# Adding up scan states: transfers that accumulate take one add of each pair, and the maxima of attention become a strand of their own

## The reference, cut to what matters

```python
dA  = exp(dt[..., None] * A)
dBx = (dt * xi)[..., None] * Bm[:, :, None, :]
def step(h, inp):
    a, bx, c = inp
    h = a * h + bx
    return (h, einsum('bds,bs->bd', h, c))
y = ys + xi * Dp
```

```python
m = max(sim, axis=-1);  e = exp(sim - m);  out = (e @ v) / sum(e)
```

## Time and profile before

| | |
|---|---|
| median of 3 runs | 3390.97 us |
| profiled execution | 3388.55 us, span 3386.7 us |
| busy share PE / DVE / ACT / POOL | 77% / 76% / 48% / 49% |
| mean granted TensorE clock | 0.802 |
| DMA engines' share, bytes | 23.4%, 253.07 MB |

### The profile page before, as it was taken

One profiled execution on the slowest core, in us unless ns is written; L12 is line 12 of the kernel. 1 busy time (PEld: TensorE's weight loads), 2 busy tenths in 40 slices (PEclk: granted clock), 3 DMA queues, 4 the chain that ended last, 5 costly groups with the idle time before them and its releaser, 6 DMA issues.

```text
span 3386.7 us, 29269 instructions
## 1 busy us (share of the span) xinstructions
PE 2602.9 (77%) x8306; PEld 846.3 (25%) x8306; DVE 2563.1 (76%) x3658; ACT 1642.3 (48%) x2312; POOL 1645.2 (49%) x1349
## 2 busy tenths in 40 slices
PE   5414465878788887988789977998589878988886
PEld 1101121223222332223222321233122322232211
DVE  1688899888788879887988888887988786346251
ACT  3434444563737474464547364556436442532523
POOL 1377676574626475455626474545736561112111
PEclk7656576799979996798779886898679876988867
DMA  2122222222313132132312231232313230102111
GB/s 80 55 81 67 76 89 88 61 87 85 101 44 92 61 117 81 64 97 70 116 38 92 83 114 55 70 91 71 124 54 107 69 109 20 60 28 80 45 35 32
DMA packets 160658, 253.07 MB, mean 75 GB/s; under 512 B 20720, under 2 KB 58480, under 8 KB 160240
## 3 DMA queue, kind: packets, MB, share of 16 engines
q1 hardware_dynamic: 160496, 251.19, 23.4%
HBM read 233.81 MB, written 16.52 MB: 74 GB/s over the span
## 4 chain that ended last, share of the span: by engine, by line
PE 46%; DVE 31%; ACT 11%; issue 8%; POOL 2%; DMA 1%; SPq 1%; DVEq 0%; POOLq 0%; ACTq 0%
PE ps L488 46%; DVE rh L1213 8%; DVE nmx L1133 5%; DVE xib L1192 3%; ACT tN L1448 3%; ACT ps L1502 2%; DVE xif L1192 2%; DVE rh L1219 2%; ACT L1250 1%; DVE tF L1074 1%; DVE tF L1079 1%; DVE tL L1121 1%; SPq L1657 1%; POOL tF L1578 1%; DVE duf L1002 0%
## 5 line engine op out<-in xcount | busy, mean ns | idle before, releaser
L1213 DVE TENSOR_TENSOR_SCAN rh<-ps,rb 128x512 f32<-128x512 f32 x512 | 622.6, 1216 | 122.4 <-ACT ps L1502 105.3
L1547 POOL TENSOR_TENSOR rh<-rh,cs 128x512 f32<-128x512 f32 x256 | 381.1, 1491 | 448.6 <-DVE rh L1213 448.5
L1133 DVE TENSOR_REDUCE nmx<-ps 128x1 f32<-128x512 f32 (+3 forms) x864 | 528.1, 660 | 59.5 <-PE ps L488 57.2
L1448 ACT ACTIVATE tN<-ps 128x1024 f32<-128x1024 f32 (+1 forms) x448 | 429.7, 959 | 258.1 <-PE ps L488 256.4
L488 PE MATMUL ps<-tN,strip 128*64 128x512 f32 (+3 forms) x2048 | 488.2, 568 | 5.3 <-DVE hN L1152 2.9
L1558 POOL TENSOR_TENSOR rb<-duf,bs 128x512 f32<-128x512 f32 x256 | 369.6, 1462 | 137.2 <-DVE rh L1213 127.8
L488 PE MATMUL ps<-hF,W 128*128 128x512 f32 x592 | 367.9, 707 | 73.1 <-DVE tF L1074 44.4
L1558 POOL TENSOR_TENSOR rb<-dub,bs 128x512 f32<-128x512 f32 x256 | 376.0, 1489 | 81.4 <-DVE rh L1213 81.0
L488 PE MATMUL ps<-Ks,Qs 48*128 48x512 bf16 (+3 forms) x1024 | 332.5, 416 | 83.8 <-DVE nmx L1133 69.1
L1572 POOL TENSOR_TENSOR tF<-tF,cr 128x512 f32<-128x512 f32 x128 | 168.7, 1320 | 392.1 <-DVE tF L1079 235.1
L488 PE MATMUL ps<-tF,W 128*128 128x512 f32 x544 | 311.6, 669 | 23.4 <-POOL tF L1578 18.2
(11 more groups left out here) (237 smaller groups left out, 3566.1 us busy)
## 6 DMA issues: line engine op xcount, KB each, us to landing
cr<-shares SPq DMA_DIRECT2D x256, 256.0 KB, 3.3
bs<-rowsf SPq DMA_DIRECT2D x128, 256.0 KB, 3.6
cs<-rowsf SPq DMA_DIRECT2D x128, 256.0 KB, 3.3
bs<-rowsb SPq DMA_DIRECT2D x128, 256.0 KB, 3.6
cs<-rowsb SPq DMA_DIRECT2D x128, 256.0 KB, 3.3
parts<-spl SPq DMA_DIRECT2D x32, 384.0 KB, 2.6
Qs<-parts SPq DMA_DIRECT2D x384, 32.0 KB
Ks<-parts SPq DMA_DIRECT2D x384, 32.0 KB
```

Source lines behind the costliest of these rows:

```text
L1133: red(nmx[:, qt, 8 * a + i:8 * a + i + k], o[:, 0:k * nk].rearrange("p (k c) -> p k c", k=k), AX.X, ALU.max, negate=True).then_inc(s_red, 1)
L1213: eng.tensor_tensor_scan(rh[n % NH][:, g, :], PS, rb[n % NBB][:, g, :], 0.0, ALU.mult, ALU.add).then_inc(s_h, 1)
L1448: act(tN[m % NP][:, :, 0:nq], PR[:, :, 0:nq], ACT.Exp).then_inc(s_ex, 1)
L1547: tt(h, h, cs[n % NB][:, :], ALU.mult).then_inc(s_cp, 1)
```

## The change

It has three parts, and the orders of SyncE, TensorE, DVE, ScalarE and POOL are written anew for them.

1. Of the 16 states of a direction, the first 14 are added up in 7 pairs (`NPAIR`). POOL issues a transfer of 128x1024 floats from the even state's tile to the odd state's tile that accumulates (`accum_op=ALU.add`), and DVE adds only the odd one to xi. The last two are added one by one. So DVE makes 9 adds for a direction in place of 16, and POOL issues 7 transfers.
2. NH is 4 in place of 3. The scan of state n now waits for state n-4: for an even one until the pair's transfer has landed (`pair_done`), for an odd one until DVE's add.
3. The maxima are a strand X with their own jobs (`jx`). Their first 8 score tiles use PA[0] and PA[1] alone, and wait, in the first tile of each bank, for the last exponential of the job ahead, not for its x. From the ninth on all three banks are used, and the first tile in PA[2] waits for that x. The output projection goes into PA[2]. The maxima are laid out so that four transfers in place of six carry them to `Qs`, two for each half of the heads, with a semaphore for each half.

```diff
-        NB, NBB, NH = 3, 2, 3
+        NB, NBB, NH = 3, 2, 4
+        NPAIR = 7
+        ADDS = NS - NPAIR
+        def pair_done(k, i):
+            m = NPAIR * k + i
+            return s_pair[m % 2], 16 * (m // 2 + 1)
+        def added(n):
+            k, s = divmod(n, NS)
+            return s_y, ADDS * k + (s // 2 + 1 if s < 2 * NPAIR else s - NPAIR + 1)
+        def state_free(n):
+            k, s = divmod(n, NS)
+            return pair_done(k, s // 2) if s < 2 * NPAIR and s % 2 == 0 else added(n)
+        FIRST = 8
+        def bank_of(u):
+            return u % 2 if u < FIRST else (2, 0, 1)[(u - FIRST) % 3]
...
+            def maxima(j, l3, before):
...
-                    if u >= 3:
-                        eng.wait_ge(s_red, tops_of(n) + u - 2)
-                    o, k = PA[u % 3], len(pieces)
+                    if last_in_bank(u) is not None:
+                        eng.wait_ge(s_red, tops_of(n) + last_in_bank(u) + 1)
+                    elif n:
+                        eng.wait_ge(*(before.dve("x") if bank_of(u) == 2 else (s_ex, units_of(n))))
+                    o, k = PA[bank_of(u)], len(pieces)
...
-                    if e == 0:
-                        eng.wait_ge(s_nm, 96 * (n + 1))
+                    if 2 * e % len(UNITS[l3]) == 0:
+                        eng.wait_ge(s_nm[g], 32 * (n + 1))
...
-                mm(R0, w(name + "o"), hN[:, :]).then_inc(*A.by_pe(j, "o"))
+                mm(O, w(name + "o"), hN[:, :]).then_inc(*A.by_pe(j, "o"))
...
                 def add_state(n):
                     k, p, s = SEQ[n]
-                    eng.wait_ge(*times_c_done(n))
-                    if s:
-                        eng.wait_ge(s_y, n)
+                    if s < 2 * NPAIR:
+                        eng.wait_ge(*pair_done(n // NS, s // 2))
                     else:
+                        eng.wait_ge(*times_c_done(n))
...
                         if n >= NH:
-                            eng.wait_ge(s_y, n - NH + 1)
+                            eng.wait_ge(*state_free(n - NH))
...
-                    if s >= 1:
-                        add_state(n - 1)
+                    if s % 2 == 0 and s >= 4:
+                        add_state(n - 3)
                         yield
                     if s == NS - 1:
-                        add_state(n)
-                        yield
+                        for m in (n - 2, n - 1, n):
+                            add_state(m)
+                            yield
...
+                def add_pair(n):
+                    k, i = n // NS, n % NS // 2
+                    eng.wait_ge(*times_c_done(n))
+                    eng.wait_ge(*times_c_done(n + 1))
+                    eng.dma_start(rh[(n + 1) % NH][:, :, :], rh[n % NH][:, :, :], accum_op=ALU.add).then_inc(
+                        s_pair[(NPAIR * k + i) % 2], 16)
...
+                    if s % 2 and 3 <= s < 2 * NPAIR + 2:
+                        add_pair(n - 3)
+                        yield
...
-                    for a in range(2):
-                        for m in range(3):
-                            dma(Qs[64 * a + 48 + m:64 * a + 49 + m, :, :],
-                                cTN[16 * m + 8 * a:16 * m + 8 * a + 8, :]).then_inc(s_nm, 16)
+                    for g in range(2):
+                        for a in range(2):
+                            dma(Qs[64 * a + 48:64 * a + 51, 4 * g:4 * g + 4, :],
+                                cTN[24 * g + 12 * a:24 * g + 12 * a + 12, :]).then_inc(s_nm[g], 16)
```

More of the change, by code:

```diff
@@ L164 @@
+        "A1S4A1S10A2S2M1F1S1F1S2F1S1F1S2F1S3F1S1F2S4F3S1F4S1F1S3A1S5A1S1A1S4A1S7A1S1A1S1M1S1A1S6F1S1F1A1S6F2S3F4M1F5A1F"
+        "2A1F1A5F2A1F14A4F1A1F3A1F2A1F2A1F8A1F3A1F5A7F3A1F2A1F3A3F8"
     ),
@@ L199 @@
     "prep3": chain("q k v bdq bdk", "q sqq k sqk v lnq rsq lnk rsk s0q s1q s0k s1k", "nq nk d0q d1q d0k d1k", ln=LN1),
-    "att2": chain("T o", "dl0 dr0 rd0 dl1 dr1 rd1", "n0 n1 n2 n3 ct on0 on1 x", ln={}),
-    "att3": chain("T o", "dl0 dr0 rd0 dl1 dr1 rd1", "n0 n1 n2 n3 ct on0 on1 x", ln={}),
+    "maxima": chain("T", "", "n0 n1 n2 n3 ct", ln={}),
+    "att": chain("o", "dl0 dr0 rd0 dl1 dr1 rd1", "on0 on1 x", ln={}),
 }
@@ L390, in build @@
                     jf[b, n] = Job(F, kind, b)
-            for b, n, kind in ((k - 3, "a3", "att3"), (k - 1, "a2", "att2")):
+            for b, n in ((k - 3, "a3"), (k - 1, "a2")):
                 if 0 <= b < B:
-                    ja[b, n] = Job(A, kind, b)
+                    ja[b, n], jx[b, n] = Job(A, "att", b), Job(X_, "maxima", b)
         for b in range(B):
@@ L472, in weights, with last_in_bank @@
             return [(g, p, t) for g in range(2) for p in range(4) for t in tiles]
+        FIRST = 8
         TOPS, UNITS = [tops(0), tops(1)], [weights(0), weights(1)]
         KINDS_A = [int(n == "a3") for _, n in ja]
+        def bank_of(u):
+            return u % 2 if u < FIRST else (2, 0, 1)[(u - FIRST) % 3]
+        def last_in_bank(u):
+            return max((v for v in range(u) if bank_of(v) == bank_of(u)), default=None)
         def tops_of(n):
@@ L720, in prep @@
                     yield
-            def attention(j, l3):
-                n, name = ATT[j.b, l3], "a3" if l3 else "a2"
-                R0, R1, O = PA
-                for s, v in j.after:
-                    eng.wait_ge(s, v)
-                if j.b == 0:
-                    eng.wait_ge(s_w[5 if l3 else 4], 16)
+            def maxima(j, l3, before):
+                n = ATT[j.b, l3]
                 for u, (pieces, nk) in enumerate(TOPS[l3]):
@@ L778, in values @@
                     eng.wait_ge(s_ex, m + 1)
+                    if e == 0 and n:
+                        eng.wait_ge(*j.after[-1])
                     if e == per:
@@ L830, in strand_f, with strand_x @@
                         yield from (ffn2 if n in ("f0", "f1") else ffn3)(j)
+            def strand_x():
+                before = None
+                for (b, n), j in jx.items():
+                    yield from maxima(j, int(n == "a3"), before)
+                    before = ja[b, n]
             def strand_a():
@@ L1234, in strand_f, with strand_x @@
                         yield from (ffn2 if n in ("f0", "f1") else ffn3)(j)
+            def strand_x():
+                for (b, n), j in jx.items():
+                    yield from maxima(j, int(n == "a3"))
             def strand_a():
```

279 lines of the change are left out of this document (148 added, 131 removed).

## The result

| | before | after |
|---|---|---|
| median of the runs, us | 3393.8 (3386.3 to 3397.4, 4 runs) | 3445.1 (3439.1 to 3451.3, 4 runs) |
| span of the profiled execution, us | 3386.7 | 3442.9 |
| mean granted TensorE clock | 0.802 | 0.790 |
| ratio after / before | | 1.0159 (95%: 1.0140 to 1.0178) |

The change makes the kernel 1.6% slower. (Before has one run more here than in the table ahead of the prediction.) I had said 3295 us, by my sum 97 us faster. The median is outside my range too (3225 to 3410).

What follows compares the result with a forecast made beforehand. No single bound: DVE paces the first stretch, DVE and PE alternate in the middle, PE mostly paces the last. From 3388.55 us, -40 - 65 - 12 - 5 + 25 = -97 gave 3291.6, stated as 3295 us; range 3225 to 3410.

Steps and rivals of the forecast that it cites:

- Part 1, adds: DVE in the scans: 112 fewer adds, 175 us less work, gaining 40 us in the first stretch and 65 in the middle.
- The gains of my sum (40, 65, 12 and 5 us): Fewer adds in the first stretch (40) and middle (65), earlier maxima in the tail (12) and middle (5).
- the transfers' 25 us: Scans waiting for pair transfers: 32 us of waiting, of which 25 us reach the end.
- near 2710: Sign to look for: the last scan begins near 2710 us in place of 2798.
- Part 3, maxima: Attention handovers: 8 reduces begin before the x of the job ahead, gaining 12 us in the tail, 5 in the middle.
- Part 2, the issue on POOL: POOL's 112 transfer issues: at 1 us each, 112 us more on POOL, hidden unless scans wait for its products.
- The rule of the Trainium skill that I weighed: POOL's transfers starved by DVE holding the shared port pair: waiting near 150 us in place of 32, result about 3400.
- Part 2, landing: Pair transfers ahead of scans: 5.5 us landing plus 1 us issue, 32 us of waiting; 91 us if 8 us.
- PE takes over: Rival, middle stretch: DVE's freed time turns idle because PE is at 83%; 3362 us, chance 0.18.
- Late transfers: Rival, first scan of even states: the pair lands late, stalling DVE's queue; near 3475 to 3545 us, chance 0.20.
- Both relieved in full: Rival: gains at full size, -76 - 129 - 30 + 20, giving 3175 us, half way 3230; chance 0.08.
- My own range: The forecast's range, 3240 to 3345 us: middle's term between 20 and 110, transfers' between 0 and 45.

Runs made afterwards that it cites:

- e1: The changed kernel without its 112 accumulating transfers, waits going to the products by C instead; 3292.6 us, 0.9704 of before.
- e13: The kernel before, in its own orders and maxima, with pairs added by POOL's accumulating transfers, issued early, and a POOL wait after each issue; 3360.9 us, 0.9900 of before.
- e11: The changed kernel with each transfer issued ahead of the product by C, and a POOL wait after each issue; 3306.4 us, 0.9743 of before.
- e9: The kernel before, in its own orders and maxima, with pairs added by POOL's accumulating transfers and a POOL wait after each issue; 3412.6 us, 1.0060 of before.
- e3: The changed kernel where POOL's second instruction after each issue waits for the first to have ended; 3356.2 us, 0.9886 of before.
- e6: The changed kernel with no transfers, DVE adding each pair itself; 3405.6 us, 1.0041 of before.
- e4: The kernel before, with POOL also issuing 112 plain 4 KB transfers between two idle tiles; 3499.4 us, 1.0316 of before.
- e2: The changed kernel with each pair's transfer replaced by a plain 512 KB copy issued from ScalarE's queue; 3281.4 us, 0.9675 of before.
- e10: The kernel before, with 112 plain 4 KB transfers issued by POOL and a POOL wait after each issue; 3431.7 us, 1.0105 of before.
- e8: The changed kernel with a POOL wait after each issue and transfers that copy instead of accumulating; 3319.4 us, 0.9776 of before.
- e5: The kernel before, with every POOL instruction waiting for the one ahead on POOL to have ended; 3417.1 us, 1.0071 of before.

## Why the prediction was wrong

- **Part 1, adds: right.** 144 adds and 216 us, where I had 144 and 225. The gains of my sum (40, 65, 12 and 5 us) can be checked together on e1, which has them and no transfer: 3293, where the sum without the transfers' 25 us was 3270. So they were some 20 us too hopeful together, within their bounds; which of them, no run tells. The last scan of e1 begins at 2707, where I had "near 2710".
- **Part 3, maxima: the mechanism right, the size open.** In the last handover of after the last exponential ends at 3285.1, and the first reduce of the next job begins 1.6 us later; in the earlier trace rows the next job had not even its first matmul for 7.3 us:

```profile
3284.09 1.02 ACT L1505 ACTIVATE tN<-ps 128x1024 f32<-128x1024 f32 x1 [0.49 <-PE ps L519]
...
3286.69 2.48 DVE L1175 TENSOR_REDUCE nmx<-ps 128x1 f32<-128x512 f32 x4 [12.38 <-PE ps L519]
...
3289.21 0.68 DVE L1196 TENSOR_TENSOR hN<-ps,rN 32x512 f32<-32x512 f32 x1
...
3290.62 1.29 DVE L1175 TENSOR_REDUCE nmx<-ps 128x1 f32<-128x512 f32 x2
...
3292.76 0.75 DVE L1206 SCALAR_TENSOR_TENSOR X<-ps,bo,X 128x512 f32<-128x512 f32 x1 [0.85 <-PE ps L519]
```

  Six reduces stand ahead of the first write of X, where I had 8. I gave the strand 17 us; with the orders it brought 54 to 56 (e13 to e11, e9 to e3), but nothing in e6, where DVE has all its work. How much of that is the strand and how much the orders is open, since no kernel has the one without the other. The 12 us for the tail are seen in after (577 us from the last scan, 590 in before), but only 5 in e11 (584).
- **Part 2, the issue on POOL: the step that failed.** "At 1 us it is 112 us more on an engine that is busy 911.7 of 1678 us (54%) in the middle, so it is hidden, as long as the products of POOL behind it are not what the scan waits for." The issue's size was right (0.871 us), and scans hardly waited for rb (6.5 us). But I asked only what POOL has to do, not what its issue does to the others. DVE's instructions with two SBUF inputs were held behind the run that follows: +112 us on the product by C alone, and 144 us of DVE's time in all (e1 to after), which I had put at nothing. DVE's queue is in order, so scans, reduces and experts behind it slipped as well. e4 shows it with no other part of the change, e1 and e2 show it gone with the transfer or with its issuer (that e2's are plain copies is not why: e4's are plain as well), and e3 and e10 show it gone, for the most part, with one wait.
- **The rule of the Trainium skill that I weighed** has the transfer starved by DVE, near 3400. What cost the time went the other way, POOL's run kept DVE out. Whether DVE also delays the transfers is open: they landed later than I took, with the hold and without it (7.4 us in after and in e3). The Trainium skill (SBUF — State Buffer, section "SBUF: two separate sides") describes the pair of ports that DVE and GpSimd share as an exclusive lock, held by the one that got there first. The trace of before agrees with that for single instructions (0.62 us mean wait for 210 cases), but for the product of state 147. In after the pair would have had to pass to DVE between POOL's instructions, as it does there nearly always, and it did not: 6.91 us for one product. The same section advises issuing from ScalarE's or SyncE's queue instead, and e2 agrees, at least for a plain copy.
- **Part 2, landing: size off, and the small cost is luck.** From the start of the issue to the landing it took 7.4 us, where I had 6.5. I had priced 32 us of stalls for 6.5 and 91 for 8, so it would be some 64 for 7.4. After shows 3.6 us, because the held DVE came late to its scans anyway: from the product of POOL to that scan it is 10.4 us at the median, and 8.4 in e1. With the hold gone the landing cost up to 37 us (e3 to e8, which has the shorter issue in it), and issuing earlier removed the stalls (e11).
- **The rivals.** "PE takes over" is out: e1, with DVE relieved, is at 3293 and not at 3362. "Late transfers" had the right side and the wrong place. "Both relieved in full" is out by e1. Against the first I had said that DVE is at 97% where PE is not full; that was one window of 40 us, and over the middle DVE is at 85%.
- **My own range** for the forecast, 3240 to 3345, was narrower than its terms: with both at their bounds it is 3224 to 3359.

What stays open: what in the hardware keeps DVE out, and why a wait on its own semaphore ends it. The records of large transfers lie over POOL's next instruction by some 0.3 us (0.87 us of issue, and the next starts after 0.61), which was one candidate; the 4 KB transfers have no such overlap (0.57 us, next start after 0.60) and hold DVE as well. Nor does it take a transfer: one product each in before and in e6 is held behind short copies of POOL. An issue makes it common (38 products over 2.6 us in after, 21 in e4, one in before), and what the two have in common is not known. That the wait ends the hold because POOL stops for a moment, and not for another reason, was not tried apart.

## What to carry to other kernels

Before POOL is given a transfer to issue, look at what POOL does right behind it: a run of computing instructions there can (here it often did) hold DVE's two-input SBUF instructions for the whole of the run. Put the issue ahead of an instruction that POOL has to wait for anyway, or let POOL wait once for its own next result, or issue from another engine's queue where the transfer allows it (here tried with plain copies alone). When DVE's busy time does not fall by what was taken off it, compare the mean and the maximum of every unchanged group: one of the same count and shape, 58% longer, is where the time went.

## What the runs showed of the hardware

- 112 transfers of 4 KB issued by POOL cost 3.2% of the kernel (e4), more than the 112 of 512 KB issued by ScalarE, which cost nothing (e2 is 0.3% below e1).
- A DVE product of 128x1024 with two SBUF inputs can be held over a whole run of POOL: 6.91 us in after behind an issue of 512 KB, 4.35 in e4 behind one of 4 KB, 5.76 in before behind two short copies and no issue.
- 512 KB within the SBUF, issue to landing, median: 7.4 us accumulating from POOL (4.4 to 9.3; 5.6 in e11), 4.8 plain from POOL, 3.0 plain from ScalarE. The Trainium skill (DMA: Bandwidth & Descriptors, section "Anatomy of one DMA — SWDGE (gpsimd) path") fits a transfer issued by GpSimd with a fixed 2 us and 436 GB/s, which would be 3.2 us by an estimate from it: POOL's plain copy takes half as long again, and its accumulating one more than twice that.
- The issue keeps POOL 0.87 us at 512 KB and 0.57 us at 4 KB, and 0.59 at 512 KB for a plain copy (e8).
- A wait of POOL on its own last result, before every instruction, costs 0.7% here (e5).
